# Graph layer on one core: replicated edge attributes loaded in five transfers of 4096-byte packets per group instead of two of 8192 and 12288 bytes

## What is computed

```python
xs, xv = split(x[dst], 64, 32);  es, ev = split(edge_attr, 8, 8)
s = einsum('ea,eb,abc->ec', xs, es, W1)*k1 + einsum('eai,ebi,abc->ec', xv, ev, W2)*k2
v = einsum('ea,ebi,abc->eci', xs, ev, W3)*k3 + einsum('eai,eb,abc->eci', xv, es, W4)*k4
messages = concat(s, v) @ Wm + bm
agg = segment_sum(messages, src, num_segments=50000)
upd = concat(x, agg) @ Wu + bu
out = layernorm(x + (x + upd))
```

## Time and profile before

| What | Value |
|---|---|
| Time, median of 3 runs | 1967.94 us (1966.78 to 1970.02) |
| The profiled execution's own time | 1963.45 us |
| Its span | 1961.8 us |
| Edge stage / node stage, by the page's slices | about 0 to 1640 us / 1700 to 1960 us |
| PE, DVE, ACT, POOL busy, share of the span | 88%, 81%, 46%, 56% |
| DMA busy, mean of 16 DMA engines, in the edge stage | 0.77 |

### The profile page before, as it was taken

One profiled execution on the slowest core, in us unless ns is written; L12 is line 12 of the kernel. 1 busy time (PEld: TensorE's weight loads), 2 busy tenths in 40 slices (PEclk: granted clock), 3 DMA queues, 4 the chain that ended last, 5 costly groups with the idle time before them and its releaser, 6 DMA issues. The chain is left out here.

```text
span 1961.8 us, 37863 instructions
## 1 busy us (share of the span) xinstructions
PE 1720.0 (88%) x11964; PEld 969.9 (49%) x11964; DVE 1583.8 (81%) x1878; ACT 908.8 (46%) x1770; POOL 1104.3 (56%) x886
## 2 busy tenths in 40 slices
PE   2644999999999999999999999999999999599995
PEld 1312444444444454444444444445444454588884
DVE  3553888888888888888888888888888885399996
ACT  1302444444444444444444444444444444277775
POOL 2104666666666666666666666666666665322221
PEclk9867999999999999999999999999999999799997
DMA  7997777777777777777777778777777774699995
GB/s 245 372 365 239 244 220 239 231 228 225 227 228 226 226 235 238 241 235 236 235 225 226 230 239 242 237 236 234 227 227 228 236 239 83 185 392 392 386 395 213
DMA packets 192108, 490.84 MB, mean 250 GB/s; under 512 B 51924, under 2 KB 104212, under 8 KB 166994
## 3 DMA queue, kind: packets, MB, share of 16 engines
q1 hardware_dynamic: 108994, 381.38, 52.3%
q0 software_dynamic: 83088, 109.13, 26.5%
HBM read 393.52 MB, written 96.88 MB: 250 GB/s over the span
## 5 line engine op out<-in xcount | busy, mean ns | idle before, releaser
L321 POOL DMA_INDIRECT agg<-summed,row_idx x392 | 640.3, 1634 | 456.9 <-DMA agg<-summed,row_idx 297.7
L506 DVE TENSOR_TENSOR prod<-ps,e_sb 128x2048 f32<-128x2048 f32 x294 | 663.6, 2285 | 136.2 <-PE ps L646 129.6
L646 PE MATMUL ps<-prod,w_sb 128*32 128x512 f32 x3136 | 753.9, 603 | 0.8 <-ACT S_sb L375 0.8
L304 POOL DMA_INDIRECT xg<-in_x_rows,dst_sb x392 | 410.7, 1048 | 187.4 <-issue 121.9
L363 ACT ACTIVATE spread<-xg 128x1536 f32<-128x1536 f32 x98 | 145.5, 1485 | 424.5 <-DMA xg<-in_x_rows,dst_sb 415.5
L514 DVE TENSOR_TENSOR prod<-ps,e_sb 128x3072 f32<-128x3072 f32 x98 | 328.0, 3347 | 0.0
L494 DVE TENSOR_TENSOR prod<-ps,e_sb 128x2048 f32<-128x2048 f32 x98 | 223.9, 2285 | 109.8 <-ACT A_sb L369 81.3
L646 PEld LDWEIGHTS ps<-prod,w_sb 128*32 128x32 f32 x3136 | 148.7, 109 | 156.4 <-issue 156.4
L627 PEld LDWEIGHTS ps<-ident_sb,spread 128*128 128x128 f32 x1176 | 127.5, 142 | 170.8 <-issue 123.0
L749 PE MATMUL ps<-wux_a,prod 128*128 128x160 f32 x784 | 180.7, 312 | 30.6 <-DVE prod L570 27.9
L639 PE MATMUL ps<-prod,w_sb 128*32 128x512 f32 x1176 | 207.4, 604 | 0.0
(11 more groups left out here) (61 smaller groups left out, 2016.8 us busy)
## 6 DMA issues: line engine op xcount, KB each, us to landing
e_sb<-in_e_rep SPq DMA_DIRECT2D x98, 1536.0 KB, 7.1
e_sb<-in_e_rep SPq DMA_DIRECT2D x98, 1024.0 KB, 5.4
agg<-start_rows SPq DMA_DIRECT2D x50, 640.0 KB, 5.0
prod<-in_x_t SPq DMA_DIRECT2D x98, 320.0 KB, 5.9
prod<-agg SPq DMA_DIRECT2D x97, 320.0 KB, 5.7
out<-prod POOLq DMA_DIRECT2D x97, 320.0 KB, 5.5
row_sb<-in_src_row SPq DMA_DIRECT2D x98, 256.0 KB
xg<-in_x_rows,dst_sb POOLq DMA_INDIRECT x392
```

What stands on the lines that cost most here:

```text
L304: nc.gpsimd.indirect_dma_start(xg[g[1] % 2][:, q, :], None, x_rows, bass.IndirectOffsetOnAxis(dst_sb[g[1]][:, q:q + 1].bitcast(U32), 0)).t ...
L321: nc.gpsimd.indirect_dma_start(agg, bass.IndirectOffsetOnAxis(row_idx[g[1]][:, q:q + 1].bitcast(U32), 0), summed[g[1]][:, q // 2, q % 2 * ...
L506: nc.vector.tensor_tensor(prod[g[1] % 2][:, 4 + 4 * i:8 + 4 * i, :].rearrange("p (a b) e -> p a b e", b=2), ps[:, t_bank(g, 1 + i), :].uns ...
L646: return nc.tensor.matmul(ps[32 * quarter:32 * quarter + 32, S_BANK, :], w[:, 32 * half:32 * half + 32], prod[g[1] % 2][:, tile, :], start ...
```

## The change

`load_e` now issues one transfer per two tiles, five in place of two. Each copies 1024 floats (4096 bytes in one piece) to each of 128 partitions, where the two before copied 2048 and 3072 floats (8192 and 12288 bytes). The first two report on `es_in` and the other three on `ev_in`, after the same waits as before, and VectorE waits for the higher counts. Bytes, buffers and all other work are the same. Lines behind L204 move down by 4.

```diff
+            def load_tiles(g, t):
+                return sp.dma_start(e_sb[g[1] % 2][:, t:t + 2, :],
+                                    e_rep[number(g), :, t:t + 2, :].unsqueeze(0).to_broadcast([32, 4, 2, GE]))
+
             def load_e(g):
                 if at_least(g, 2):
 
                     sp.wait_ge(multiplied, number(g) * USES - 2 * USES + 4)
-                sp.dma_start(e_sb[g[1] % 2][:, 0:4, :], e_rep[number(g), :, 0:4, :].unsqueeze(0).to_broadcast([32, 4, 4, GE])
-                             ).then_inc(es_in[g[1]], 16)
+                for t in range(0, 4, 2):
+                    load_tiles(g, t).then_inc(es_in[g[1]], 16)
                 if at_least(g, 2):
                     sp.wait_ge(multiplied, number(g) * USES - 2 * USES + 6)
-                sp.dma_start(e_sb[g[1] % 2][:, 4:ET, :], e_rep[number(g), :, 4:ET, :].unsqueeze(0).to_broadcast([32, 4, ET - 4, GE])
-                             ).then_inc(ev_in[g[1]], 16)
+                for t in range(4, ET, 2):
+                    load_tiles(g, t).then_inc(ev_in[g[1]], 16)
...
-                dve.wait_ge(es_in[g[1]], g[0] * 16 + 16)
+                dve.wait_ge(es_in[g[1]], g[0] * 32 + 32)
...
-                    dve.wait_ge(ev_in[g[1]], g[0] * 16 + 16)
+                    dve.wait_ge(ev_in[g[1]], g[0] * 48 + 48)
```

## The result

| What | Before | With the change |
|---|---|---|
| Time, median (lowest to highest) | 1968.98 us (1966.78 to 1971.47) | 1991.53 us (1984.72 to 1993.5) |
| Ratio, 95% interval | | 1.0138 (1.0089 to 1.0187) |
| The profiled execution's own time / span | 1963.45 / 1961.8 us | 1991.22 / 1989.6 us |

The change makes the kernel slower, by about 1%; forecast was 4.7% faster. A later series of the same kernel gave 1984.06 us (1981.09 to 1988.11), ratio 1.0078 (1.0057 to 1.0098), so the loss lies between 0.6 and 1.9%.

The account below looks back on a forecast made before the run. GpSimd's chain of scatters was taken to bound the edge stage. 1963.45 - 89 + 0 + 1 - 4 = 1871.5 us for the profiled execution, 1876 for the median (-4.7%); range 1867 to 1940.

Parts of the forecast that it names:

- What bounds the kernel: Edge stage: GpSimd's chain of scatters makes one group in three take 17.51 us; TensorE and VectorE set the 14.81 floor.
- Smaller pieces in front of the scatters: GpSimd's scatters in the edge stage: each waits behind one 0.524 MB piece only, so slow groups reach 14.81 us: -89 us.
- theory A: Follow-up runs' expectation, order of arrival: a scatter waits for everything that reached its DMA engine earlier, and for nothing later.
- three waits: GpSimd's waits for landing scatters in three groups, 3.20, 2.90 and 2.38 us, each to leave 1.45 at most.
- budget of 7.6 us: GpSimd's waits in three groups beyond the usual 0.30 us; saving 2.9 of them was to be enough.
- Packets (0): DMA engines: 384 more packets per group cost near 0 each, at most 151 ns, covered by idle DMA time: 0 us.
- SyncE's queue (0): Three more issues of 0.55 us per group fall into SyncE's existing waits; later edge attributes still arrive in time: 0 us.
- Start (+1): Until 162 us, DMA saturated by the fill of `agg`: six groups' pieces add 1 us (0 to 22).
- End (-4): After the last row indices, four pairs of scatters follow; a faster chain catches up: -4 us, between 0 and -12.
- Block and dearer packets: Rival at GpSimd's three waits: queued pieces stay one block, each packet's extra time lengthens the wait: 1993 us, chance 0.10.
- nothing: Rival: all queued pieces go as one block, so scatters wait as long as before: 1968 us, chance 0.10.
- Part of the gain: Rival: pieces queue before a scatter comes, some DMA engines take two together, half the wait goes: 1923 us, chance 0.20.

Follow-up runs that it names:

- the best version: Kernel before, two transfers, each load made to wait for a one-element GpSimd store (the mark) after a pair of scatters: 1865.31 us, ratio 0.9475.
- the two kernels with loads ahead: Against the kernel before, a GpSimd semaphore increment behind each pair released loads just ahead of its second scatter: 2118.8 us with two transfers, 2068.0 with five.
- those with loads between the scatters: Against the kernel before, the releasing increment moved behind the pair's two gathers; loads came between the scatters: 2289.57 us with two transfers, 2191.73 with five.
- the pile-up at 7.67: Kernel before plus GpSimd's store after each pair, only the second load waiting for it; two loads stood ahead of one pair: 2110.65 us, ratio 1.0710.
- the one kernel that tried it: Kernel before with 24 more instructions in SyncE's queue ahead of the second load, nothing split: 1912.75 us, ratio 0.9703.

## Why the prediction was wrong

- **What bounds the kernel: right.** GpSimd's chain of scatters holds the stage, the loads make it late, and the floor is 14.81 us. Without loads, and with both loads held by marks, all groups take 14.81. In the best version the last row indices come at 1582.38 us in place of 1671.30, 88.9 us earlier: the -89 of the sum, by another way.
- **Smaller pieces in front of the scatters (-89): wrong, and the whole error.** Two steps failed. The first: "I take a scatter or gather to wait for the transfer that its DMA engine is in, and not for those of SP's queue behind it". With loads issued just ahead of a pair, pieces took 0.37 us off the landing where 2.07 were forecast (6.12 to 5.75, not 4.05). What came before a scatter goes before it, nearly all of it. This order of arrival fits the landings of all these runs in kind: the first row of the table (one piece issued ahead of the end of the scatter's issue, the second behind or close to it), the two kernels with loads ahead, those with loads between the scatters, and the pile-up at 7.67. It was fitted after the fact: the times that theory A gave beforehand missed in most runs, since the places of the loads were not known. The Trainium skill (DMA: Bandwidth & Descriptors, section on queues, rings and completion order) describes turns between queues with up to 64 descriptors at a time; the near block of three pieces agrees with its long end, which the prediction priced at 0 and then gave a chance of 0.10.
- The second: that three waits shrink and no others come. Where the scatter did get ahead of pieces, by 1.0 us in the first row, the pieces it passed stood ahead of the next pair, which had been mostly free: 3.37 to 4.44 us (4.13 in the later series). The prediction's budget of 7.6 us of waits in three groups had no row for the pairs that were free, and they had the most to lose: waits in 1200 us went from 81 to 114. These two steps show why the gain of 89 us did not come. Why it became a loss of 1% stays open: the loss comes with the split of the second transfer (+1.0% alone), packets do not account for it, and a later issue made things better, not worse, in the one kernel that tried it.
- **Packets (0): right for the time.** 9 to 15 ns a packet on the DMA engines, nothing in the kernel's time. The forecast of near 0, from an equal 43 us per MB at two mixes of packets, was too low by that much, and the bound of 151 ns far too wide.
- **SyncE's queue (0): right as cover,** the extra issues went into the waits of L212 and L198. But that a load comes later or earlier by a microsecond was treated as free because its data are not needed for long. It moves the load against the pairs, and that is what decides here: 1865 to 2290 us for the same two transfers.
- **Start (+1): right,** the first scatter starts at 164.79 us, before at 162.98 (in the later series at 162.81). **End (-4): did not come,** four pairs still follow the last row indices, since the chain got no faster. Where it did, in the best version, three follow in place of four, and the last pair starts at 1594.81 in place of 1692.61, 9 us more than the 88.9; the term was within its bounds.
- **The rivals.** "Block and dearer packets" gave 1993, which the first series nearly met (1991.5), by a cause that the packets alone refute. Its first half, the block, is what the runs with loads ahead show; from the block alone "nothing" follows, and the 1% over it comes from the second transfer's pieces, in a way not shown. "Part of the gain" had the right reason, that more than one piece is queued before a scatter comes; only the first transfer's split alone shows some gain (-0.7%), and a small one.
- A sign that was there: the table's rows of before. Sorting its pairs by where the load was issued shows landings of 2.9, 4.7 and 5.7 us, and that a shift of a microsecond is worth as much as the piece size. The prediction read three pairs and took them for all.

## What to carry to other kernels

Where a chain of short dependent transfers shares DMA engines with bulk loads, first sort the chain's waits by when the loads were issued, and count the links that don't wait: these are what a change can lose. Then place the loads, before thinking of cutting them. In the fastest kernel here the longer load came right behind a pair, and no pair had two loads between it and the one before. Hold every load in its place: with one left free the pattern settled at +7.1% in place of -5.3%.

## What the runs showed of the hardware that was not expected

- **A semaphore increment in GpSimd's program runs ahead of the indirect DMAs before it:** SyncE's load came 0.44 us into the first of two scatters that the increment stands behind. The completion of a store of one number, 0.61 us, marks the place instead: the load came 0.16 us after it.
- **Transfers to 64 partitions are slower:** 768 KB took a median of 10.1 us to land, which includes standing behind another half, where 1536 KB to 128 partitions took 7.1; the queue's time rose by 43%, and the kernel lost 20.7%. It agrees with the Trainium skill (SBUF — State Buffer, section on the DMA port swizzle), by which partitions 0 to 63 are reached by only half of the 16 ports.
- **The same program can take clearly different times:** single runs of 1894.7 among nine at 1967, and 1960.8 among six at 1906 to 1938. That their loads stood differently against the pairs is likely, and not shown. A median of a few runs can hide it.
- **Pieces in front of a scatter count almost as one transfer would:** landing after 5.75 us behind three, 6.12 behind one of the same size.
